# Gate input of a Mamba and expert block summed by TensorE in PSUM and copied by ScalarE; one state's product with C moved from GpSimd to VectorE

## What is computed

```
xn = layernorm(x)
# selective scan, forwards and on the reversed sequence, 16 states each
dbc = xn @ x_proj_w.T -> delta (rank 32), B (16), C (16)
delta = softplus(delta @ dt_proj_w.T + dt_proj_b)
h[t] = exp(delta*A) * h[t-1] + delta*B*x        # for each of 16 states
s = sum over states (h * C) + D*x               # both directions added
# expert block; expert sel chosen per row from its last token
h1 = gelu(xn @ W1[sel] + b1[sel])
f  = (h1 @ W2[sel] + b2[sel]) @ Wo + bo
g  = silu(xn + 0.3*f)
out = x + s * g
```

## Time and profile before

| | before |
|---|---|
| median of 3 runs | 3112.79 us (3112.57 to 3116.84) |
| profiled execution | 3118.2 us, its span 3116.4 us |
| busy: DVE | 3021.6 us, 97% |
| busy: POOL | 3013.3 us, 97% |
| busy: ACT | 2940.6 us, 94% |
| busy: PE | 2489.1 us, 80% |
| granted TensorE clock, mean | 0.958 of full |
| DMA | 394.17 MB, 126 GB/s |

### The profile page before, as it was taken

How to read it: one execution, slowest core, us unless ns; L and a number is a source line. 1 busy time by engine, 2 the same in 40 slices (tenths; PEclk the granted TensorE clock), 3 DMA queues, 4 the chain that set the end, 5 groups by cost and what they waited for, 6 DMA issues and landing times. The chain is left out here.

```text
span 3116.4 us, 49216 instructions
## 1 busy us (share of the span) xinstructions
PE 2489.1 (80%) x15990; PEld 1970.9 (63%) x15990; DVE 3021.6 (97%) x1995; ACT 2940.6 (94%) x5242; POOL 3013.3 (97%) x1486
## 2 busy tenths in 40 slices
PE   7878878878778888788787788887788887887886
PEld 6666656666656666566666566666666665666665
DVE  3999999999999999999999999999999999999999
ACT  5899999999999999999999999999999999999995
POOL 3899999999999999999999999999999999999997
PEclk9999999999999999999999999999999999999998
DMA  5543334444334444344433444443444433444331
GB/s 174 151 134 116 125 119 130 143 125 119 118 123 141 135 124 123 111 131 143 130 120 119 127 128 140 127 124 111 128 139 134 126 120 114 131 144 130 107 122 55
DMA packets 273364, 394.17 MB, mean 126 GB/s; under 512 B 45003, under 2 KB 119508, under 8 KB 273108
## 3 DMA queue, kind: packets, MB, share of 16 engines
q1 hardware_dynamic: 273108, 391.03, 41.1%
HBM read 348.98 MB, written 25.18 MB: 120 GB/s over the span
## 5 line engine op out<-in xcount | busy, mean ns | idle before, releaser
L480 POOL TENSOR_TENSOR bx<-dx,b_sb 128x1024 f32<-128x1024 f32 x576 | 1362.9, 2388 | 10.2 <-DVE hs L861 9.5
L861 DVE TENSOR_TENSOR_SCAN hs<-decay,bx 128x1024 f32<-128x1024 f32 x576 | 1308.7, 2277 | 8.7 <-ACT decay L682 4.3
L468 POOL TENSOR_TENSOR hc<-hs,c_sb 128x1024 f32<-128x1024 f32 x480 | 1135.7, 2376 | 22.6 <-DVE hs L861 21.1
L1091 PE MATMUL y<-ident,hc 128*128 128x128 f32 x8192 | 1068.6, 277 | 36.0 <-DVE hc L840 36.0
L1091 PEld LDWEIGHTS y<-ident,hc 128*128 128x128 f32 x8192 | 942.0, 143 | 148.5 <-DVE hc L840 106.0
L861 DVE TENSOR_TENSOR_SCAN hs<-decay_sb,decay 128x1024 f32<-128x1024 f32 x448 | 1004.7, 2266 | 11.8 <-issue 10.5
L682 ACT ACTIVATE decay<-delta,rate 128x512 f32<-128x512 f32 x1152 | 745.6, 684 | 38.8 <-DVE hs L861 35.9
L594 ACT ACTIVATE dxb<-dxT,btok 128x256 f32<-128x256 f32 x1792 | 759.2, 503 | 0.3 <-PE decay L1066 0.3
L1066 PE MATMUL decay<-ident,dxb 128*128 128x128 f32 x3584 | 477.2, 276 | 244.9 <-DVE hs L861 212.8
L840 DVE TENSOR_TENSOR hc<-hs,c 128x1024 f32<-128x1024 f32 x544 | 649.6, 1194 | 1.3 <-issue 0.7
L1066 PEld LDWEIGHTS decay<-ident,dxb 128*128 128x128 f32 x3584 | 396.5, 141 | 401.3 <-issue 259.1
(11 more groups left out here) (125 smaller groups left out, 2050.8 us busy)
## 6 DMA issues: line engine op xcount, KB each, us to landing
b_sb<-b_scratch SPq DMA_DIRECT2D x576, 256.0 KB, 3.3
c_sb<-b_scratch SPq DMA_DIRECT2D x480, 256.0 KB, 3.5
xin<-in_L_attn_x_dram SPq DMA_DIRECT2D x32, 512.0 KB, 6.6
w_sb<-in_L_ffn_W_dram SPq DMA_DIRECT2D x32, 512.0 KB, 3.4
w2o_sb<-w2o_scratch SPq DMA_DIRECT2D x32, 512.0 KB
xres<-in_L_attn_x_dram SPq DMA_DIRECT2D x32, 512.0 KB, 5.4
out_dram<-og SPq DMA_DIRECT2D x32, 512.0 KB, 4.3
dbc<-high SPq DMA_DIRECT2D x64, 128.0 KB, 2.3
```

The lines of the kernel that those rows point to most:

```text
L468: nc.gpsimd.tensor_tensor(hc[:, s % RING, :, :], hs[:, s % HSLOTS, :, :], c_sb[:, i % CRING, :].unsqueeze(1).broadcast_to([P, DT, T]), ALU ...
L480: nc.gpsimd.tensor_tensor(bx[:, i % RING, :, :], dx[:, g, :, :], b_sb[:, i % BRING, :].unsqueeze(1).broadcast_to([P, DT, T]), ALU.mult).th ...
L861: V.tensor_tensor_scan(hs[:, s % HSLOTS, :, :].rearrange("p k t -> p (k t)")[:, u], factor.rearrange("p k t -> p (k t)")[:, u], data.rearr ...
L1091: ins = M(yps[:, c, k * P:(k + 1) * P], hc[:, s % RING, k, c * P:(c + 1) * P], ident[:, :], start=False, stop=(s == ADDED[-1]), is_transpo ...
```

## The change

PE adds xn into the `front` bank with one float32 matmul against the identity for each of the four token blocks of a row, so that the bank holds the finished gate input. ACT copies it out in two units at the same step numbers at which DVE made it before. The factor 0.3 moves into W2*Wo when it is copied at the start, and into its bias. State 26 leaves `POOL_C`, so its product with C goes from POOL to DVE, its C from a DMA to a PE broadcast.

```
-    POOL_C, C_LAG, ADD_LAG = (2, 4, 5, 7, 9, 10, 11, 12, 16, 18, 20, 22, 24, 26, 27), 4, 2
+    POOL_C, C_LAG, ADD_LAG = (2, 4, 5, 7, 9, 10, 11, 12, 16, 18, 20, 22, 24, 27), 4, 2
...
# ACT: new, called from drain() at steps GATE (GATE_FIRST in row 0), ahead of the step's decay
+            def gate_input(row, v):
+                act.wait_ge(s_pf, row * UNITS + 12 + v)
+                if v == 0:
+                    wait(act, s_yg, row)
+                A(zz[:, 2 * v:2 * v + 2, :], fps[:, :].rearrange("p (c d) -> p c d", c=2), ACT.Copy).then_inc(s_zz, 1)
...
# ACT: copy_w2o
-                  ACT.Copy).then_inc(s_w2oc, 1)
+                  ACT.Copy, scale=FFN_SCALE).then_inc(s_w2oc, 1)
...
# DVE: removed
-            def gate_input(row, v):
-                dve.wait_ge(s_pf, row * UNITS + 12 + v)
-                if v == 0:
-                    wait(dve, s_yg, row)
-                V.scalar_tensor_tensor(zz[:, 2 * v:2 * v + 2, :], fps[:, :].rearrange("p (c d) -> p c d", c=2), 0.3,
-                                       xn[:, 2 * v:2 * v + 2, :], ALU.mult, ALU.add).then_inc(s_zz, 1)
...
# DVE: once, at the start
+            V.tensor_scalar(bias_sum, bias_ps[0:NE, 0:D], FFN_SCALE, None, ALU.mult).then_inc(s_biass, 1)
...
# PE: ffn_out, after the last part of a token block
-                    ins = M(to, ones3[:, :], bias3[:, :], start=False, stop=True)
+                    M(to, ones3[:, :], bias3[:, :], start=False, stop=False)
+                    ins = M(to, ident[:, :], xn[:, c, :], start=False, stop=True)
```

More of the change, by code:

```diff
@@ L59, in mamba_moe_block @@
     AHEAD, AHEAD_NEXT = {5: 8, 14: 22, 15: 24, 16: 26, 23: 28, 26: 29, 27: 30}, {29: 5}
-    EPS = 1e-5
+    EPS, FFN_SCALE = 1e-5, 0.3
     LN_SCALE, LN_SHIFT = 0.6110144853591919, 0.6499999761581421
@@ L164, in mamba_moe_block @@
         wo_sb = decay_sb[:, 1, 1, :].rearrange("p (k n) -> p k n", k=DT)
-        bo_row, bias_rest, bias_rest2 = dxb[0:1, 0, 0, :], dxb[0:NE, 0, 1, :], dxb[0:NE, 0, 2, :]
+        bo_row, bias_rest, bias_rest2, bias_sum = dxb[0:1, 0, 0, :], dxb[0:NE, 0, 1, :], dxb[0:NE, 0, 2, :], dxb[0:NE, 0, 3, :]
         w2_in = (w2o_sb, xres)
@@ L202, in mamba_moe_block @@
         s_bias, s_biasc, s_biasst, s_b2T, s_dtz = (sem(n) for n in ("bias_ready", "bias_parts", "bias_stored", "b2T_loaded", "dtw_zeroed"))
+        s_biass = sem("bias_scaled")
         s_proj, s_bstored = sem("projected_copied"), sem("b_stored")
@@ L653, in drain @@
                     hidden(row, HIDDEN.index(s))
+                at = GATE if row else GATE_FIRST
+                if s in at:
+                    gate_input(row, at.index(s))
             def front(row, par, s):
@@ L822, in front @@
                     low_part(row)
-                at = GATE if row else GATE_FIRST
-                if s in at:
-                    gate_input(row, at.index(s))
             def output(row):
@@ L918, in _ @@
             dve.wait_ge(s_bias, 1)
-            bias_sum = bias_ps[0:NE, 0:D]
+            V.tensor_scalar(bias_sum, bias_ps[0:NE, 0:D], FFN_SCALE, None, ALU.mult).then_inc(s_biass, 1)
+            dve.wait_ge(s_biass, 1)
             V.tensor_copy(bias_part[:, 0, :], bias_sum).then_inc(s_biasc, 1)
             dve.wait_ge(s_biasc, 1)
-            V.tensor_tensor(bias_rest[:, :], bias_sum, bias_part[:, 0, :], ALU.subtract).then_inc(s_biasc, 1)
+            V.tensor_tensor(bias_rest[:, :], bias_sum[:, :], bias_part[:, 0, :], ALU.subtract).then_inc(s_biasc, 1)
             dve.wait_ge(s_biasc, 2)
```

## The result

| | before | changed |
|---|---|---|
| median | 3114.82 us | 3166.89 us |
| ratio | | 1.0163, 95% interval 1.0143 to 1.0183 |
| profiled execution, its span | 3118.2 us, 3116.4 us | 3168.72 us, 3166.9 us |
| DVE, POOL, ACT, PE busy | 97, 97, 94, 80% | 96, 93, 94, 82% |

The kernel before was run once more beside the changed one, which moves its median from 3112.79 to 3114.82 us. The change makes the kernel 1.6% slower, some 52 us, where 64 us was forecast. One of the changed kernel's four runs, 3247.99 us at a mean granted clock of 0.838, was disturbed and is not in the ratio.

A forecast was written before the change was run, and what follows sets the result against it. DVE was taken to set the pace, with PE full behind the Gelu. 28 us for the gate region plus 36 us for state 26's product gave 64 us on 3112.8 us: 3177 us, range 3132 to 3208 us.

The forecast's parts named there:

- The bound: Whole kernel: DVE sets the pace and the others follow; PE has no room for some 20 us behind the Gelu.
- The backlog in the late row: PE's queue behind the Gelu: added matmuls delay state 6's transposes by 1.41 us and state 8's by 1.88 us.
- the late row: Profiled batch row at 1023.69, where scan 6 starts only 0.14 us after its data; scan 13 forecast 1.05 us late.
- The gate term: Gate region, scans 6 to 13: PE's added matmuls cost 0.9 us a row, bounds 0 and 1.5 us; 28 us together.
- the early one: The next profiled row, where state 6's transposes have 1.25 us of lead; scan 13 forecast 0.55 us late.
- The product of state 26: On DVE between scans 27 and 28, where it does not wait: costs 1.12 us a row in full, 36 us.
- ACT's copies inside PE's delay: ACT's queue ahead of scan 13: its two copies make it 1.0 us late, covered by 1.4 us from PE.
- Break-even in the gate region: Rival, chance 0.2: PE's queue closes up, scan 13 comes when it did, only the new product counts; 3149 us.
- a change that DVE's sum decides: Rival, chance 0.10: PE and ACT keep up, DVE's lighter work and ended waits make it faster; 3086 to 3097 us.
- The clock rival: Rival, chance 0.12: PE's half-clock stretch behind the Gelu grows, costing about 1.5 us more a row; 3224 us.

The follow-up runs named there:

- the gate change alone: The changed kernel with state 26's product back on GpSimd, so only the gate input is changed: 3143.33 us, ratio 1.0084.

## Why the prediction was right, and where its sizes were off

**The bound.** Right. DVE sets the pace, and PE, 80% busy on average, had nothing to spare behind the Gelu. The run without identity matmuls undoes the gate part at the same clock, and cheaper transposes in the same place undo it too.

**The backlog in the late row.** Right to within 0.1 us up to scan 7, in a row of the same clock: transposes for state 6 forecast 1046.42, found 1046.38; scan 6 1046.42 and 1046.41; scan 7 1048.66 and 1048.61. Scan 8 was forecast 1052.37 and came at 1052.60, because of a wait that I had not priced: the spread of C for state 6 stands behind the same backlog, and the product of state 6 waits 0.58 us for it. Scan 13 was forecast 1.05 us late and is 1065.67 - 1064.85 = 0.82 us late. The forecast had ACT's queue add 0.45 us between scans 8 and 13, and here it adds nothing: scan 8 is 0.81 us late already. ACT was 1.17 us late at xnT, not 1.4, and 0.34 us of slack leaves 0.83 us, no more than DVE's own delay.

**The gate term, 0.9 us a row.** Within the changed kernel it is 0.38 us, and this is the term that was mis-sized. Two things make the difference. First, the price at a given place of the clock's rise was put too high at both ends: 0.82 us for the late row where 1.05 was forecast, and 0.2 to 0.3 us for rows like the early one where 0.55 was forecast; and the mean was then taken near the late row. Second, I took for fixed how often a row is late, and that follows from the length of the row: one row in four of the kernel before is like the late row, and one in five of the changed kernel, with the others mostly earlier. Measured as a difference, the gate change costs 25 us alone and 22 us on top of the moved product (3166.89 - 3145.08). That this is near the forecast's 28 us is partly luck, since the 25 us come from rows in step with the clock, which the forecast did not have.

**The product of state 26, 1.12 us a row.** Right at its place, 1.11 us at scan 28, in the changed kernel and in both with state 26 alone. As a difference it made 27 us, not 36 us, since the row that it lengthens meets the clock's rise early.

**ACT's copies inside PE's delay.** Right, and shown by the run without identity matmuls. ACT's queue is the next limit: it takes 0.73 us as soon as PE is on time.

**The rivals.** Break-even in the gate region, and a change that DVE's sum decides, did not come about. But the second is close: with the backlog relieved, the gate change alone is 0.2 to 0.4% faster than before. The page of the Trainium skill that pointed to it (Perfetto Trace Analysis, Optimizing Scalar/DVE Operations) is borne out by three runs here, once TensorE's share in the critical stretch is made smaller. The clock rival was half seen: the mean granted clock fell from 0.958 to 0.942. But the half-clock stretch behind the Gelu does not end later than before (at most 12.7 us behind scan 0, before 12.8), and the drops that have come in lie in the middle of a row and near its end, where DVE did not wait for PE in this kernel.

## What to carry to other kernels

An engine that is 80% busy can be full for 20 us of each period; price new work by the stretch in which it lands, and put what does not depend on the late input ahead of the wait for it. Where TensorE's granted clock changes within a period, measure each half of a change alone and with a small filler. A wait that grows with the place of the clock's rise can give back what is added elsewhere, so that costs neither add nor subtract as the rows suggest. And moving work can move the clock's rise as well; look at the granted clock before calling the gain one of place.

## What was not expected of the hardware

TensorE's clock does not rise at a fixed place of the program: in the kernel before it rises 9.5, 10.7, 11.9 and 12.6 us behind scan 0 in turn. In the gate change alone the program fell into step with it, rows of 95.57 us with the rise at the same place to 0.1 us in all but a few. Adding 0.33 us of VectorE work to each of 32 rows changed the time by -1.2 us, nothing clear of noise, where the same work cost 12.7 us in a kernel without such a wait.

Two matmuls moved ahead of the Gelu were worth as much as leaving out all four: each gave back 25 us of 3167 us. In the row shown they fill TensorE's idle time there at half clock, and the eight matmul records behind the Gelu then take 2.33 us for 3.75 us. In both runs it is ScalarE that holds scan 13, at the same place to 0.01 us.
